# Layer 0 of a two-layer transformer kernel: heads stacked in pairs on partition halves, whole-row maxima, projection and attention in one block

## The reference, cut to what matters

```python
# x is (2, 1024, 256); 16 heads of 16
q = (layernorm(x) @ Wq + bq), split in heads
k, v = (layernorm(x) @ Wkv + bkv), split in heads
q, k = q * scale, k * scale
q, k = apply_rotary(q, x), apply_rotary(k, x)   # rotation, times the norm of x's row
qn, kn = layernorm(q, ln_h_g, ln_h_b), layernorm(k, ln_h_g, ln_h_b)   # over the 16 of a head
logits = einsum('bhqd,bhkd->bhqk', qn, kn) / sqrt(16)
att = softmax(logits)                            # 1024 x 1024 for each of 32 heads
a = einsum('bhqk,bhkd->bhqd', att, v)
```

## Time and profile before

| | |
|---|---|
| Median of 3 runs | 2167.97 us (2162.94 to 2171.13) |
| Profiled execution, its own time | 2167.56 us |
| Span of its trace | 2165.9 us |
| TensorE busy over the span | 89% |
| VectorE / ScalarE / GpSimd busy | 68% / 56% / 41% |
| Granted TensorE clock, mean | 0.943 of full speed |

### The profile page before, as it was taken

How to read it: one execution, slowest core, us unless ns; L and a number is a source line. 1 busy time by engine, 2 the same in 40 slices (tenths; PEclk the granted TensorE clock), 3 DMA queues, 4 the chain that set the end, 5 groups by cost and what they waited for, 6 DMA issues and landing times. The chain is left out here.

```text
span 2165.9 us, 40750 instructions
## 1 busy us (share of the span) xinstructions
PE 1929.3 (89%) x11376; PEld 1297.2 (60%) x11438; DVE 1472.4 (68%) x3391; ACT 1222.2 (56%) x2508; POOL 896.3 (41%) x905
## 2 busy tenths in 40 slices
PE   4997999999959759999739899999998999999998
PEld 1452333333237659999725477777754777777787
DVE  4896888888548859999539576677365565653442
ACT  0683777777735237777314467767344777773331
POOL 1341000000027757798244187887300666662300
PEclk7895999999979979999969899999998999999999
DMA  7963000000072258899522011211101011111000
GB/s 205 289 145 59 2 0 0 1 0 1 1 203 96 98 172 265 265 282 279 178 66 61 4 47 42 57 45 49 35 1 39 24 25 35 25 35 39 11 10 20
DMA packets 185944, 173.87 MB, mean 80 GB/s; under 512 B 19651, under 2 KB 170741, under 8 KB 184822
## 3 DMA queue, kind: packets, MB, share of 16 engines
q1 hardware_dynamic: 173750, 143.23, 23.9%
q0 software_dynamic: 10720, 29.44, 4.1%
q10 hardware_dynamic: 1376, 0.02, 0.0%
HBM read 96.15 MB, written 61.60 MB: 73 GB/s over the span
## 5 line engine op out<-in xcount | busy, mean ns | idle before, releaser
L2633 POOL TENSOR_TENSOR w_rest<-work,w_head 128x512 fp32r<-128x512 f32 (+3 forms) x384 | 395.4, 1044 | 212.6 <-ACT w_head L2598 205.1
L767 DVE TENSOR_REDUCE half_max<-m_ps 128x1 f32<-128x512 f32 x512 | 317.4, 684 | 58.1 <-PE m_ps L689 57.7
L824 ACT ACTIVATE weights<-s_ps 128x512 f32<-128x512 f32 x512 | 266.2, 600 | 108.1 <-PE s_ps L707 108.1
L2594 ACT ACTIVATE work<-s_ps 128x512 f32<-128x512 f32 (+3 forms) x384 | 187.5, 488 | 113.2 <-PE s_ps L2423 91.1
L2598 ACT ACTIVATE w_head<-work 128x512 fp32r<-128x512 f32 (+3 forms) x384 | 201.4, 524 | 72.9 <-PE o_ps L2433 65.8
L689 PE MATMUL m_ps<-kT,qT 96*128 (+1 forms) x512 | 204.3, 400 | 8.4 <-DVE half_max L767 6.4
L707 PE MATMUL s_ps<-qT,kT 99*128 (+1 forms) x512 | 193.3, 384 | 9.5 <-DMA qT<-max_rows 5.1
L2433 PE MATMUL o_ps<-w_head,lat_head 128*128 128x512 f32 (+3 forms) x384 | 177.9, 463 | 7.1 <-POOL w_rest L2633 7.1
L864 POOL COPY v_now<-v 128x83 f32 (+1 forms) x64 | 16.0, 256 | 366.6 <-PE o_ps L719 361.7
L2474 DVE CUSTOM_DVE_ANT_0 work<-m_ps,mask_row 128x128 bf16<-128x128 f32 (+3 forms) x256 | 120.3, 485 | 49.2 <-PE m_ps L2391 46.2
L1072 POOL TENSOR_TENSOR gv_rest<-ex_wgv,gv_head 128x736 fp32r<-128x736 f32 x64 | 114.3, 1786 | 69.4 <-ACT gv_head L1169 69.4
(11 more groups left out here) (404 smaller groups left out, 5044.3 us busy)
## 6 DMA issues: line engine op xcount, KB each, us to landing
slots<-zero SPq DMA_DIRECT2D x8, 3456.0 KB, 27.5
rows<-slots SPq DMA_DIRECT2D x64, 256.0 KB, 3.4
slots<-ex_out SPq DMA_DIRECT2D x64, 256.0 KB, 3.0
ex_wgv<-in_L_ffn_wg_dram SPq DMA_DIRECT2D x72, 176.0 KB, 3.0
ex_wgv<-in_L_ffn_wv_dram SPq DMA_DIRECT2D x72, 176.0 KB, 3.3
ex_wo<-in_L_ffn_wo_dram SPq DMA_DIRECT2D x72, 128.0 KB, 3.2
oT<-work SPq DMA_DIRECT2D x64, 128.0 KB
w_down<-l_inverse SPq DMA_DIRECT2D x32, 256.0 KB, 3.9
```

The lines of the kernel that those rows point to most:

```text
L767: dve.tensor_reduce(half_max[:, u:u + 1], m_ps[:, BANK[u], :], AX.X, ALU.max).then_inc(max_done, 1)
L824: act.activation(w[:, s % 2 * 4 + j, :], s_ps[:, BANK[4 * s + j], :], ACT.Exp, scale=HD ** -0.5).then_inc(w_done, 1)
L2594: act.activation(w[:, s % 3, c0:512], s_ps[:, s % 3, c0:512], ACT.Exp, scale=SM1).then_inc(d["w_done"], 1)
L2633: pool.tensor_tensor(w_rest[:, s % 3, c0:512], w[:, s % 3, c0:512], w_head[:, s % 3, c0:512], ALU.subtract).then_inc(d["w_rest_done"], 1)
```

## The change

`l0_project` and `l0_attend` become one function, `l0_heads`, in one block with no meeting between projection and attention.

- q and k are split in two fp32r parts instead of three bf16 ones: 3 products of 16 rows and 2 rows for the maximum, 50 rows a head instead of 99. Even heads lie on partitions 0 to 63, odd ones on 64 to 127, so a transpose turns two heads (16 fp32 transposes a tile instead of 32 in bf16), and ScalarE evacuates two double banks instead of four.
- The two gains move from VectorE to GpSimd (`gains`), which also makes both rests; ScalarE copies one part (`heads`). VectorE's sum of the rotation's two parts keeps its place on VectorE (`rotated`), ahead of `scale`; `centre` comes behind `scale`.
- The bias is added by an fp32r matmul over 33 rows (the bias in two parts). Two operations on one row and four on GpSimd prepare it.
- The doubling of the parts (`double`) is four DMAs for each batch. The placing (`place`) is two DMAs for 512 queries.
- A maximum is taken over a whole row of 1024 keys, two banks at once (`maximum`), 32 a group. `m_ps` is a ring of two double banks that row scores and turns (of maxima and of outputs) share in a fixed order, `l0_ring`; `LEAD` is 12 steps. Maxima are split on GpSimd (`parts`).
- In a step the row scores alternate with the scores on the other partition half.
- v is read where it lies, without a copy to `v_now`. The groups of the attention are written out, not looped over.

```diff
+            dve.tensor_copy(bias_qkv[0:1, :], bias_in[0:1, :]).then_inc(split, 1)
+            dve.tensor_tensor(bias_qkv[BIAS_REST:BIAS_REST + 1, :], bias_in[0:1, :], bias_qkv[0:1, :], ALU.subtract)
...
+def l0_ring():
+    ring = []
+    def units(step):
+        ring.extend(("unit", n) for n in (2 * step, 2 * step + 1) if n < NG * NU)
+    for step in range(LEAD):
+        if step == 9:
+            ring.append(("turn", 0))
+        units(step)
+    for step in range(STEPS):
+        if step % 8 == 5:
+            ring.append(("turn", step // 8 + 1))
+        units(step + LEAD)
+    ring.append(("turn", 2 * NG + 1))
+    return ring
...
+                double(0)                       # SP
+                place(0)
+                double(1)
+                for n in range(1, 2 * NG):
+                    place(n)
...
-                for u in range(2):              # VectorE
-                    dve.memset(stack[:, u, :, :], 1.0).then_inc(ones_done, 1)
...
+                def rotated(t, u):
                     dve.wait_ge(own_done, t + 1)
                     dve.wait_ge(oth_done, 2 * t + 2)
-                    reuse(dve, p1_done, t, 2)
-                    reuse(dve, r1_done, t, 2)
+                    reuse(dve, rest_done, t, 2, 2)
                     dve.tensor_tensor(val[:, u], own[:, u], oth[:, u], ALU.add).then_inc(rot_done, 1)
...
+                def maximum(n):
+                    g, half, qt, pair, odd = unit_of(n)
+                    if n % HALF == 0 and n >= NU:
+                        dve.wait_ge(parts_done, n // HALF - 1)
+                    dve.wait_ge(m_done, n + 1)
+                    dve.tensor_reduce(row_max[:, half, qt, odd, pair:pair + 1], m_ps[:, PLACE["unit", n] % 2], AX.XY,
+                                      ALU.max).then_inc(max_done, 1)
...
                     if more:                    # VectorE's step
+                        rotated(t + 1, 1 - u)
+                    else:
+                        maximum(1)
+                    scale(t, u)
+                    if more:
                         centre(t + 1, 1 - u)
-                    scale(t, u)
+                    if isinstance(t, int) and t == T - 2:
+                        maximum(0)
...
+                def gains(t, u):                # GpSimd
+                    pool.wait_ge(unit_done, t + 1)
+                    pool.tensor_tensor(own[:, u, 0:H0, :], val[:, u, 0:H0, :],
+                                       g_h[:, :].unsqueeze(1).to_broadcast([P, H0, HD]), ALU.mult
+                                       ).then_inc(gain_done, 1)
+                    pool.wait_ge(gain_done, t + 1)
+                    pool.tensor_tensor(val[:, u, 0:H0, :], own[:, u, 0:H0, :],
+                                       b_h[:, :].unsqueeze(1).to_broadcast([P, H0, HD]), ALU.add
+                                       ).then_inc(val_done, 1)
+                def rests(t, u):
+                    pool.wait_ge(head_done, t + 1)
+                    for i, part in ((0, q_stack[:, :, 1, :]), (1, k_stack[:, :, 2, :])):
+                        side = slice(H0 * i, H0 * i + H0)
+                        pool.tensor_tensor(part.bitcast(F32R), val[:, u, side], stack[:, side, 0, :], ALU.subtract
+                                           ).then_inc(rest_done, 1)
...
+                pool.memset(stack[:, :, :, :], -1.0).then_inc(preset, 1)
                 pool.memset(v[:, :, :, :], 1.0).then_inc(v_ones, 1)
...
+                        for i in range(4):      # ScalarE's step of the attention
+                            weight(g, s, i)
+                            if i == 1 and s % 8 == 5 and 2 * g + s // 8 + 1 < 2 * NG:
+                                copy_shift(2 * g + s // 8 + 1)
...
+                def free(at):                   # TensorE: is the ring's double bank free
...
+                    kind, n = RING[at - 2]
+                    if kind == "unit":
+                        pe.wait_ge(max_done, n + 1)
+                        return
+                    if n < 2 * NG:
+                        pe.wait_ge(sh_copied, n + 1)
+                    if n >= 2:
+                        pe.wait_ge(att_done, n - 1)
...
+                    if isinstance(t, int) and t == T - 1:
+                        for n in range(2):
+                            for kh in range(2):
+                                row_scores(n, kh)
...
+                for n in range(2, 4):
+                    for kh in range(2):
+                        row_scores(n, kh)
                 turn_stack(T - 1, 1)
+                for kind, n in RING[4:2 * LEAD + 1]:
+                    if kind == "unit":
+                        for kh in range(2):
+                            row_scores(n, kh)
+                    else:
+                        turn(n)
+                pe.wait_ge(evacuated, 2 * T)
+                for g in range(NG):
+                    for s in range(16):
+                        at = 16 * g + s
+                        ahead = 2 * (at + LEAD)
+                        more = ahead < NG * NU
+                        if s % 8 == 5:
+                            turn(2 * g + s // 8 + 1)
+                        for i in range(4):
+                            if i >= 2 and more:
+                                row_scores(ahead + 1, i - 2)
+                            scores(g, s, i)
+                            if i < 2 and more:
+                                row_scores(ahead, i)
+                        if at > 0:
+                            outputs(at - 1)
```

More of the change, by code:

```diff
@@ L24 @@
 H0, HD = 16, 16
-NP = 6
-QK0 = NP * HD
-ROWS0 = QK0 + 3
+SLOT0 = 64
+QK0 = 3 * HD
+ROWS0 = QK0 + 2
 NG = B * H0 // 4
@@ L315, in l0_project @@
         eps = l.sb("eps", [P, 1])
[L316 to L323, removed]
[L324 to L327 removed]
+        row_max = l.sb("row_max", [P, 2, 4, 2, 2])
@@ new lines, in rests, with step @@
+                def rests(t, u):
[4 more added lines that the diff above has]
+                                           ).then_inc(rest_done, 1)
+                def step(t, u, b):
+                    gains(t, u)
+                    rests(t, u)
@@ L475, in _ @@
+                pool.memset(stack[:, :, :, :], -1.0).then_inc(preset, 1)
+                pool.memset(v[:, :, :, :], 1.0).then_inc(v_ones, 1)
+                pool.wait_ge(both_done, 2)
+                steps(pool, step)
+                for n in range(2 * NG):
+                    parts(n)
             @block.scalar
@@ new lines, in row_scores @@
+                def row_scores(n, kh):
+                    g, half, qt, pair, odd = unit_of(n)
+                    at = PLACE["unit", n]
+                    if kh == 0:
+                        if n in (0, 4 * NU):
+                            pe.wait_ge(duplicated, DOUBLED * (n // (4 * NU) + 1))
+                        free(at)
+                    queries, keys = rows_of(qT, g, pair, odd, QK0), rows_of(kT, g, pair, odd, QK0)
+                    tile = (4 * half + qt) * P
+                    i = pe.matmul(m_ps[:, at % 2, kh, :], queries[:, tile:tile + P], keys[:, kh * 512:kh * 512 + 512],
+                                  start=True, stop=True)
+                    if kh == 1:
+                        i.then_inc(m_done, 1)
@@ new lines, in outputs @@
+                def outputs(at):
+                    g, half, kt = at // 16, at % 16 // 8, at % 8
+                    pe.wait_ge(w_done, 4 * at + 4)
+                    if kt == 0 and at > 0:
+                        pe.wait_ge(o_copied, 2 * g + half)
+                    for j in range(4):
+                        i = pe.matmul(o_ps[32 * j:32 * j + 32, :], v[:, g, kt, VW * j:VW * j + 32],
+                                      w[:, at % 2 * 4 + j, :], start=kt == 0, stop=kt == TB - 1, skip_group_check=True)
+                    i.then_inc(pv_done, 1)
@@ L883, in layer0_attention @@
+                outputs(STEPS - 1)
+                turn(2 * NG + 1)
 def layer0_attention(nc, m, c, a, work, x_dram, loaded, slots, zero, cleared):
```

538 lines of the change are left out of this document (206 added, 332 removed).

## The result

| | before | after |
|---|---|---|
| Median | 2168.14 us (2162.30 to 2173.98, 20 runs) | 2174.99 us (2168.37 to 2180.70, 20 runs) |
| Ratio | | 1.0031 [1.0023, 1.0039] |
| Profiled execution, own time | 2167.56 us | 2180.45 us |
| Mean granted clock of the span | 0.943 | 0.926 |

The account below looks back on a forecast made before the run. TensorE bounds the first tiles, VectorE later ones; VectorE is near its limit in attention, above a TensorE-ScalarE floor. Gains of 16 (projection), 13 (hand-over) and 39.5 (steps) make 68.5: 2167.6 to 2099 us, range 2070 to 2156.

Parts of the forecast that it names:

- Start: Block's start: two memsets leave VectorE, two one-row copies come (2 us); net 3.7 us sooner, GpSimd's new memset costing nothing.
- First tiles: Projection at half clock: the cheaper bias matmul makes a tile 8.2 us instead of 10.3, three tiles 6 to 7 shorter.
- Later tiles: Rest of the projection: 6.6 us a tile instead of 6.95, 4 us gained over 12 tiles (bounds 11 gained, 15 lost).
- The ring of 6.6 us through GpSimd: Projection tile: unit values, gains, copy, subtractions, sum and normalising close over one tile, 6.6 us (6.0 to 8.2).
- Hand-over: VectorE's projection end to first scores: about 30.5 us instead of 43.6, 13 us gained (bounds 8 to 17).
- Steps, pairs: Attention steps: a scores matmul runs beside a row-score one on the other partition half, 0.23 us a pair.
- the pairs one after another: Rival for the attention steps: paired matmuls run in turn, step 2.92 us, 2155 us in all; chance 0.13.
- Steps, the plain step: Attention step without a turn: the loop of TensorE and ScalarE sets a floor of 2.40 us, for 128 steps.
- The rival by the Trainium skill's rule on weight loads: Rival for the steps: loads overlap only matmuls of another row group; 0.2 us more a step, 2124 us; chance 0.08.
- Steps, the turn: Once in eight attention steps: 1.1 us for transposes and 1.25 for row scores waiting on ScalarE's copy of the maxima.
- Steps, the clock: Attention steps: full clock, with 3 us for cold steps; rival of half clock, 4.0 us a step, 2310 us, chance 0.09.
- The 43 cold steps: Half-clock rival in the attention: at 1.6 us each, it decides from 43 cold steps on, against 68.5 us to lose.

Follow-up runs that it names:

- 8: The changed kernel with ScalarE copying the turned maxima ahead of its first exponential in the turn step; 2133.71 us, 0.9828 against the kernel before.
- 2: The changed kernel with q, k and the placed maxima stored in bf16 instead of fp32r; 2121.19 us, 0.9795 against the kernel before.

## Why the prediction was wrong

- *Start: failed.* "The new GpSimd memset ... so nothing; uncovered, under 1 us" cost 4.9, and it wasn't `stack`'s memset alone: that of v, in the same queue, held VectorE too. (5.4 less 2 is 3.4 and not 3.7, but the two copies took 1.5; without the memsets in the way the first x came 5.4 sooner than before.) The Trainium skill, "SBUF — State Buffer", Who interferes with whom, says that a VectorE operation such as `tensor_scalar` can ask for a port pair that GpSimd holds for a whole instruction, and then stands fully. The 6.26 us beside the memsets and 0.17 without them agree; that it stood through a second one, which began 1.7 us after it, is this trace's.
- *First tiles: better than forecast,* 6.92, 6.95 and 7.69 for 8.2. The granted clock was at 1.00 in part of them, from 39.8 us on, where before it stood at 0.50 until 70.8; that wasn't counted.
- *Later tiles: failed.* The ring of 6.6 us through GpSimd was real as a bound (6.5 came out once it was the longest), but the step missed a longer one: one `stack` in place of two, with `heads` ahead of v's copy in ScalarE's queue. 7.8 at full clock and 9.4 at half instead of 6.6; with the first tiles 19 us over. I had counted the operations that ScalarE loses, not what stands behind the one that now waits.
- *Hand-over: held in its sum,* 3.3 over; its parts were 2.5 and 2.2 over and 1.5 under.
- *Steps, pairs: held.* Scores and row scores do start hundredths apart, and neither the pairs one after another nor VectorE decides.
- *Steps, the plain step: mis-sized.* 2.40 was read from bf16 rows, and fp32r has 0.1 more at two places of the loop: 0.2 x 128 = 26 us. The rival by the Trainium skill's rule on weight loads named 2.60 as well, but by two loads for one half of the array; the step is 2.60 with no row scores too, so that reason isn't the one. The earlier trace rows were read rightly and used wrongly: they show a load hidden under a running matmul, and the loop's loads come where none is running.
- *Steps, the turn: held* in size, 2.21 for 2.35, fourteen times and not fifteen.
- *Steps, the clock: failed.* "3 for cold steps" were about 26: 9 behind five turns, 13 in the tail of this execution, and 4 in the first eight steps, where the first turn is one of the six with a fall. I had weighed the clock for the steps as a whole, all cold or all warm. It falls in places: behind some stalls of 1.25 to 1.40 us, and in some executions where the work thins out. That the stall has part in it is shown by 8, where both are gone; that it isn't enough is shown by 2, where stalls of 1.41 us had no fall behind them. The 43 cold steps that would undo everything weren't needed, since the other terms had been eaten already.

24 for start and tiles, 3 for the hand-over, 47.5 for the steps and 7 of scatter make the 81. What stays open is which of load and matmul makes the 0.1, why the clock falls after one stall and not after the next, and why after none in bf16.

## What to carry to other kernels

When a buffer loses its second copy, write down for the engine that now waits what stands behind the wait in its queue, and who waits for that; here a copy of 0.37 us that waited for nothing itself came 3.5 us late behind another, and the tile took 7.8 us where 6.5 was possible. Take a loop's latencies from rows of the same number type, and look whether a load stands behind a wait or under a matmul. A short stall on TensorE can cost more in granted clock than in itself (here 1.2 us, and 1.5 or 2.4 in the groups where the clock fell behind it), so a small copy belongs ahead of the long work of its engine when the engine is idle anyway.

## What was not expected of the hardware

A VectorE operation of 0.17 us stood 6.26 us, through two GpSimd memsets in a row and not only the one that ran when it began. Moving one 0.57 us copy of ScalarE raised TensorE's granted clock from 0.57 to 1.00 in the steps behind a turn, while in bf16 the clock stayed at 1.00 behind fourteen stalls of 1.2 to 1.41 us. In the tail the granted clock stayed at 1.00 in one execution of the changed kernel, with TensorE busy for 14.28 of 17 us, and at 0.50 in another, with the same work.
